# Interleaving the high and low rows of q and k in DRAM, and moving value tiles, one weight piece, zero fills and reflections in the order of work

## What is computed

```
x = x + gate * proj(attention(modulate(layernorm(x))))      # block 0, 16 heads of 18
x = x + gate * moe(modulate(layernorm(x)))                  # 4 experts, top 2 of them per token, hidden 1152, gelu
x = x + gate * attention(...);  x = x + gate * mlp(...)     # block 1: the same with one dense MLP
x_rot = x + ((x U) expm(A(cond)) - x U) U^T                 # block 2: U from qr(P), P 288 x 64; A skew-symmetric 64 x 64
x = x + gate * attention(...);  x = x + gate * mlp(...)     # block 3: layernorm with weights, exact gelu
```

## Time and profile before

| | us |
|---|---|
| median of 3 runs (lowest, highest) | 1743.58 (1736.67, 1746.56) |
| profiled execution | 1738.26 |
| its span | 1736.5 |
| PE busy | 1596.7 |
| DVE busy | 1095.3 |
| ACT busy | 942.5 |
| POOL busy | 607.3 |
| longest idle time of PE | 10.31, at 504 to 515 |

### The profile page before, as it was taken

How to read it: one execution, slowest core, us unless ns; L and a number is a source line. 1 busy time by engine, 2 the same in 40 slices (tenths; PEclk the granted TensorE clock), 3 DMA queues, 4 the chain that set the end, 5 groups by cost and what they waited for, 6 DMA issues and landing times.

```text
span 1736.5 us, 27878 instructions
## 1 busy us (share of the span) xinstructions
PE 1596.7 (92%) x9537; PEld 1040.5 (60%) x9537; DVE 1095.3 (63%) x2236; ACT 942.5 (54%) x1696; POOL 607.3 (35%) x1349
## 2 busy tenths in 40 slices
PE   7899989998979999997799999899988999998998
PEld 5334445446768888886335454489864354443897
DVE  4757777747535446564786877544447878784544
ACT  2456555566545455563365766744432667676442
POOL 1246576556245547554374742110001012101100
PEclk9789999899989999999699999999986999999999
DMA  6643434433464454441442222220203322222000
GB/s 193 189 133 102 149 112 156 140 129 103 163 207 131 147 179 149 158 145 46 147 127 84 85 66 86 73 60 1 47 27 114 107 82 90 70 83 73 18 28 28
DMA packets 101039, 183.44 MB, mean 106 GB/s; under 512 B 12141, under 2 KB 54520, under 8 KB 100786
## 3 DMA queue, kind: packets, MB, share of 16 engines
q1 hardware_dynamic: 90158, 145.97, 26.5%
q0 software_dynamic: 8352, 33.20, 6.1%
q10 hardware_dynamic: 2388, 2.48, 0.5%
HBM read 133.18 MB, written 60.05 MB: 111 GB/s over the span
## 4 chain that ended last, share of the span: by engine, by line
PE 67%; DVE 12%; DMA 8%; ACT 5%; issue 4%; POOL 2%; SPq 2%; DVEq 0%; ACTq 0%; POOLq 0%
PE ps L1328 14%; PE ps L1339 13%; PE ps L1186 7%; PE ps L1175 7%; PE ps L1064 6%; DVE mx L2036 5%; PE ps L1115 4%; PE ps L1162 3%; PE ps L1071 2%; DMA qk_rows<-qk 2%; PE ps L1104 2%; DMA w2raw<-in_w 2%; PE ps L1085 1%; PE ps L1078 1%; DMA qs<-nmT 1%
## 5 line engine op out<-in xcount | busy, mean ns | idle before, releaser
L2036 DVE TENSOR_REDUCE mx<-ps 128x1 f32<-128x512 f32 x768 | 481.5, 681 | 70.3 <-PE ps L1162 67.9
L1622 ACT ACTIVATE pT<-ps 128x512 f32<-128x512 f32 x768 | 410.1, 602 | 185.8 <-PE ps L1175 184.7
L1162 PE MATMUL ps<-ks,qs 54*128 54x512 f32 x768 | 299.3, 493 | 25.5 <-DMA ks<-qk_rows 16.2
L1175 PE MATMUL ps<-qs,ks 56*128 56x512 f32 x768 | 277.1, 463 | 14.9 <-DMA qs<-nmT 6.0
L1970 DVE TENSOR_TENSOR gl<-gf,gh 128x512 fp32r<-128x512 f32 x171 | 118.9, 696 | 194.0 <-ACT gh L1536 192.9
L1175 PEld LDWEIGHTS ps<-qs,ks 56*128 56x128 f32 x768 | 119.4, 192 | 178.8 <-issue 92.7
L1186 PE MATMUL ps<-pT,vaug 128*32 128x512 f32 x1536 | 214.4, 627 | 6.3 <-ACT pT L1622 6.3
L1339 PE MATMUL ps<-w2h,gh 128*128 128x288 f32 x684 | 206.5, 302 | 2.8 <-DVE tmpx L2070 1.9
L1339 PE MATMUL ps<-w2l,gh 128*128 128x288 f32 x684 | 201.8, 295 | 0.0
L1339 PE MATMUL ps<-w2h,gl 128*128 128x288 f32 x684 | 201.4, 294 | 0.0
L790 POOL TENSOR_SCALAR nwp<-mvp 128x4 f32<-128x4 f32 x21 | 4.1, 195 | 518.2 <-DVE mvp L1855 517.8
(11 more groups left out here) (293 smaller groups left out, 3044.3 us busy)
## 6 DMA issues: line engine op xcount, KB each, us to landing
qk_rows<-qk SPq DMA_DIRECT2D x96, 252.0 KB
w1raw<-in_w SPq DMA_DIRECT2D x39, 576.0 KB, 4.2
w2raw<-in_w SPq DMA_DIRECT2D x39, 432.0 KB, 4.9
qs<-qk_rows SPq DMA_DIRECT2D x96, 144.0 KB
ks<-qk_rows SPq DMA_DIRECT2D x96, 144.0 KB
expert_out<-expert_out POOLq DMA_DIRECT2D x8, 1152.0 KB, 7.1
htok<-expert_rows SPq DMA_DIRECT2D x11, 768.0 KB, 6.3
qs<-qk_rows SPq DMA_DIRECT2D x96, 72.0 KB
```

What stands on the lines that cost most here:

```text
L1162: ins = mm(bank(n), qs[at:at + KMAX, buf, h // 2, qt * P:(qt + 1) * P], ks[at:at + KMAX, buf, h // 2, :], start=True, stop=True, tile_posi ...
L1175: ins = mm(bank(n), ks[at:at + KROW, b % 2, h // 2, kt * P:(kt + 1) * P], qs[at:at + KROW, b % 2, h // 2, :], start=True, stop=True, tile_ ...
L1622: A(pT[:, kt % 2 * HG + i, :], bank(BANK[when[0], "score", (g, kt, i)]), ACT.Exp, scale=SCALE).then_inc(S["exp_done"], 1)
L2036: V.tensor_reduce(mx[:, g % NG, qt, column(i):column(i) + 1], bank(BANK[when[0], "max", (g, qt, i)]), AX.X, ALU.max).then_inc(S["mx_done"], 1)
```

## The change

The DRAM tensor `qk_rows` gets the shape heads x 18 x 2 x 512 in place of heads x 2 x 18 x 512: high and low row of one channel lie side by side. `rows_of` now names the rows of one part as one list with a fixed stride. `load_rows` takes, for `qs`, 36 interleaved rows and 18 high rows; for `ks`, the 18 high rows twice (into even and odd partitions) and the 18 low rows: with both halves of the partitions 10 DMAs per stack in place of 8, and `STACK_LOADS` (160) in place of 128 in the waits. At an opening the four value tiles stand between q/k tiles 1 and 2, on TensorE, on DVE and in the table of banks. For expert tile 3 the rows are loaded after the first weight piece, with the wait for the zero fills; two fills follow the first weight piece of tile 2, one each the second and the third. The reflections of expert tiles 7 and 10 move to other hidden tiles.

```diff
--- before.py
+++ after.py
@@ -54,7 +54,7 @@
 
 FWD_STEP = {(0, 0): (2, 5, 7, 9, 11, 14), (0, 1): (0, 2, 5, 7, 10, 12, 14), (0, 2): (0, 3, 5, 7, 10, 12, 14), (0, 3): (2, 5, 8, 11, 14),
             (1, 1): (0, 2, 4, 6, 9, 11, 13), (1, 2): (0, 2, 4, 6, 9, 11, 13)}
-FWD_TILE = ((3,), (), (0, 3, 6), (0, 3, 6), (0, 3, 6), (0, 3, 6), (0, 4), (2, 5), (0, 4), (0, 3, 6), (2, 5, 8))
+FWD_TILE = ((3,), (), (0, 3, 6), (0, 3, 6), (0, 3, 6), (0, 3, 6), (0, 4), (3, 7), (0, 4), (0, 3, 6), (1, 4, 8))
 
 
 def reflections_in(l, b):
@@ -99,7 +99,7 @@
 ROUTE_LATE = {(0, 5, "B"): [("T2", 0)], (0, 6, "B"): [("T2", 1)], (0, 7, "B"): [("T2", 2)], (0, 8, "B"): [("lg", 0)],
               (1, 0, "A"): [("back", 0)], (1, 0, "B"): [("back", 1)], (1, 1, "B"): [("lt", 0), ("top2", 0)], (1, 2, "A"): [("back", 2)],
               (1, 2, "B"): [("back", 3)], (1, 3, "B"): [("pos", 0)], (1, 4, "B"): [("list", 0)]}
-FILL_AT = ((0,), (1, 2), (3,))
+FILL_AT = ((0, 1), (2,), (3,))
 for i_, part_ in enumerate(MOD_PARTS):
     ROUTE_LATE.setdefault((3 + i_ // 4,) + ((1, "A"), (2, "A"), (2, "B"), (4, "B"))[i_ % 4], []).append(("M", (1,) + part_))
 for u_ in range(2):
@@ -194,10 +194,12 @@
         phase = ("start", l)
         for c in range(KC):
             take(phase, "T1", c)
-        for tile in range(QT - 1):
+        for tile in range(2):
             take(phase, "P", tile)
         for t in range(TT):
             take(phase, "V", t)
+        for tile in range(2, QT - 1):
+            take(phase, "P", tile)
         if l != 1:
             take(phase, "M", (l, 1))
             for u in range(2):
@@ -243,6 +245,7 @@
 KMAX = 3 * HD
 KROW = KMAX + 2
 HEAD = (1, 0, 3, 2)
+STACK_LOADS = 2 * 5 * 16
 
 
 def weights_at(j, first, last, ahead):
@@ -275,7 +278,7 @@
 def bass_cond_seq_kernel(nc, a, out):
 
     modd = nc.dram_tensor("mod_rows", [NL, B, MOD], F32).ap()
-    qkd = nc.dram_tensor("qk_rows", [2 * NH, 2, HD, N], F32).ap()
+    qkd = nc.dram_tensor("qk_rows", [2 * NH, HD, 2, N], F32).ap()
     wpd = nc.dram_tensor("proj_rows", [NL, C, C], F32).ap()
     vd = nc.dram_tensor("skew_rows", [B, RD * RD], F32).ap()
     hd = nc.dram_tensor("expert_rows", [IDLE * N, KC * P], F32).ap()
@@ -460,17 +463,21 @@
 
         def rows_of(tile, part):
 
-            return qkd[HT * tile:HT * tile + QR[tile] // HD, part], qk[0:QR[tile], tile % 2, part, :].bitcast(F32)
+            rows = qkd[HT * tile:HT * tile + QR[tile] // HD, :, part].rearrange("h d n -> (h d) n")
+            return rows, qk[0:QR[tile], tile % 2, part, :].bitcast(F32)
 
         def load_rows(eng, i, g, which):
 
             o = 2 * HG * g
-            for to, row, src in (((qs, 0, qkd[o:o + HG]), (qs, 2 * HD, qkd[o:o + HG, 0:1])),
-                                 ((ks, 0, qkd[o + HG:o + 2 * HG, 0:1]), (ks, HD, qkd[o + HG:o + 2 * HG])))[which]:
-                for e in range(2):
-                    part = src.rearrange("(p e) a d n -> e (a d) p n", e=2)[e]
-                    at = HALF * e + row
-                    eng.dma_start(to[at:at + part.shape[0], i % 2, 2 * g:2 * g + 2, :].bitcast(F32), part).then_inc(S[f"stack_ld{g}"], 16)
+            to, first = ((qs, o), (ks, o + HG))[which]
+            heads = qkd[first:first + HG].rearrange("(p e) d a n -> e d a p n", e=2)
+            for e in range(2):
+                high, low = heads[e, :, 0], heads[e, :, 1]
+                both = heads[e].rearrange("d a p n -> (d a) p n")
+                for at, step, src in ((0, 1, both), (2 * HD, 1, high)) if to is qs else ((0, 2, high), (1, 2, high), (2 * HD, 1, low)):
+                    rows = src.shape[0]
+                    start = HALF * e + at
+                    eng.dma_start(to[start:start + step * (rows - 1) + 1:step, i % 2, 2 * g:2 * g + 2, :].bitcast(F32), src).then_inc(S[f"stack_ld{g}"], 16)
 
         @block.sync
         def _(sp):
@@ -514,7 +521,7 @@
                     o = HT * tile
                     if i:
                         for g in range(o // (2 * HG), (o + QR[tile] // HD - 1) // (2 * HG) + 1):
-                            sp.wait_ge(S[f"stack_ld{g}"], i * 128)
+                            sp.wait_ge(S[f"stack_ld{g}"], i * STACK_LOADS)
                     for part in parts:
                         sp.wait_ge(S[("hi_done", "lo_done")[part]], i * QT + tile + 1)
                         sp.dma_start(*rows_of(tile, part)).then_inc(S[f"qk_st{tile % 2}"], 16)
@@ -656,9 +663,8 @@
                     load_projection(l + 1)
                 for k in range(1, TILES if l == 0 else 0):
                     if k > 1:
-                        if k == PICKED[2]:
-                            sp.wait_ge(S["zf_done"], NE * 16)
-                        load_tokens(k)
+                        if k != PICKED[2]:
+                            load_tokens(k)
                         e = expert_of(k)
                     if k > 1:
                         sp.wait_ge(S["gh_done"], NJ * (k - 1) + 3)
@@ -672,6 +678,9 @@
                         sp.wait_ge(S["fc1_mm"], NJ * (k - 1) + NJP * (q + 1))
                         sp.wait_ge(S["fc2_mm"], NJ * (k - 1) + NJP * (q + 1) + 3)
                         load_piece(w1, w2, q)
+                        if (k, q) == (PICKED[2], 0):
+                            sp.wait_ge(S["zf_done"], NE * 16)
+                            load_tokens(k)
                         for n in FILL_AT[q] if k == PICKED[2] - 1 else ():
                             sp.wait_ge(S["tl_ready"], 3)
                             sp.wait_ge(S["zb_ready"], 1)
@@ -1154,7 +1163,7 @@
                 def max_tiles(g, qt, which):
 
                     if qt == 0 and which[0] == 0:
-                        pe.wait_ge(S[f"stack_ld{g % NG}"], 128 * (it + g // NG + 1))
+                        pe.wait_ge(S[f"stack_ld{g % NG}"], STACK_LOADS * (it + g // NG + 1))
                     for i in which:
                         n = bank_free("max", (g, qt, i), "mx_done", G * NU + (NU * g + qt * HG + i + 1))
                         h = (g % NG) * HG + HEAD[i]
@@ -1253,10 +1262,12 @@
                     for c in range(KC):
                         turn_layernorm(1, c, it)
                     pe.wait_ge(S["wq_ready"], l + 1)
-                    for tile in range(QT - 1):
+                    for tile in range(2):
                         qk_tile(it, tile)
                     for t in range(TT):
                         v_tile(t)
+                    for tile in range(2, QT - 1):
+                        qk_tile(it, tile)
                     if l != 1:
                         if l == 0:
                             pe.wait_ge(S["ld_adar"], 32)
@@ -2114,11 +2125,13 @@
                     when[0] = ("start", l)
                     for c in range(KC):
                         split_h1(it, c)
-                    for tile in range(QT - 1):
+                    for tile in range(2):
                         low_part(it, tile)
                     dve.wait_ge(S["ld_w"], 16 * (l + 1))
                     for t in range(TT):
                         v_out(t)
+                    for tile in range(2, QT - 1):
+                        low_part(it, tile)
                     if l != 1:
                         modulation_half_out(l, 1, BANK[when[0], "M", (l, 1)])
                     if l == 0:
```

## The result

The kernel after took 1738.49 us (median of 20 runs, 1728.73 to 1745.49), the kernel before beside it 1744.9 us (20 runs, 1736.67 to 1757.28). The ratio is 0.996, 95% interval 0.9943 to 0.9977: 7.0 us faster (4.0 to 9.9), where 12.8 us had been forecast. The gain has the forecast's sign and the time lies in its range; the size was about half.

The account below looks back on a forecast made before the run. TensorE, busy 92% of the span, was taken to bound the kernel, so only its idle time could be saved. Gains of 2.5 + 2.0 + 0 + 6.0 + 2.3 = 12.8 us off 1743.58 gave 1730.8 us, range 1720 to 1741.

Parts of the forecast that it names:

- part 1: Stores of q/k rows: DMA share from 0.44 to about 0.88, landing 2.8 us earlier in the opening of layer 1.
- Rival 1: Stores of q/k rows get no faster, limited by something other than the number of engines: 1739.8 us; chance 0.13.
- part 2: Stack loads: 10 DMAs instead of 8, same bytes, cost SP 0.73 us more a stack; last load lands as much later.
- Rival 4: SP's queue: 35 us of extra issuing over 48 stacks makes it slower, 1752.7 us if 30 hand on delay; chance 0.07.
- Opening of layer 1, 2.5 us: First stack 2.1 us earlier (store -2.8, loads +0.73), second 0.4 more: 2.5 us gained.
- Elsewhere, 2.0 us: Waits for `nmT` and small stack waits outside layer 1's opening: chains 0.7 us shorter each, 2.0 us gained in all.
- Value tiles, 0: Value tiles between the q/k tiles at an opening: no gain and no cost.
- Expert tile, 6.0 us: Fourth expert tile: first weight piece issued 5.1 us earlier, rows landing just in time; 6.0 us gained.
- Rival 2: Rows of the fourth expert tile arrive last, turned at 510.3: gain 2.8 instead of 6.0 us, 1734.0 us; chance 0.12.
- Reflections, 2.3 us: Expert tile 7: the 3.82 us wait goes, 1.1 to 1.5 us come late next; gain 2.3 us, tile 10 nothing.
- Rival 3: More than the sum: shorter pauses leave TensorE's clock high and layer chains give all: 20 us, 1723.6 us; chance 0.13.
- Signs named beforehand: Wrong if the store's landing does not move, rows arrive after 508, or new waits for `nmT` appear in the layers.

Follow-up runs that it names:

- old_opening: Kernel after with the value tiles of an opening behind all q and k tiles again: 1717.8 us, 0.9904 of the kernel before on chip C.
- experts_only: Kernel before with only the fourth expert tile's edit, the zero fills and the moved reflections: 1731.3 us, 0.9986 of the kernel before on chip C.
- after_fourth: Kernel after, unchanged, run once more on chip E: 1715.1 us, 0.9878 of the kernel before.

## Why the prediction was wrong in size

**Stores (part 1): right.** Share 0.82 where 0.88 was expected, the landing 3.2 us nearer to the last issue where 2.8 was. From the last store's issue to the first load it is 2.5 us for 5.7; in the other profiles 2.6 to 3.1 us with the new rows and 4.7 to 5.8 with the old. Rival 1 (stores no faster) fell. By the section of the Trainium skill quoted there, "Why a DMA increments its semaphore by 16 and not by 1" in "DMA: Bandwidth & Descriptors", the share would be 14 of 16, 0.88, in place of 7 of 16, 0.44; the traces' 0.82 and 0.44 agree with it to 0.06.

**Loads (part 2): the price was mis-sized.** "2 x 0.37 = 0.73 us more" took the issue time of the old form for the new one. It is about 2.9 us a stack: 5.9 us for ten (1.41 + 4.44) against 2.94 for eight. The sum didn't suffer as feared, for two reasons: the opening's first wait ends with a landing that issuing doesn't set alone (5.51 us with cheap loads on chip E, 5.65 with dear ones; from the last load's issue to TensorE's start it was 3.66 us before and is 1.91 now), and stores give 0.9 us of SP a tile back. The wait for `nmT` near 127 us may be a trace of the price: 1.4 to 1.9 us in the eight profiles with ten loads, 0.5 to 1.7 in the four with six, 0 to 1.4 in the seven with the old rows. Rival 4 (SP's queue) fell, although its price was four times what it had assumed.

**Opening of layer 1, 2.5 us: right, with some luck.** The two waits fell by 4.4 us from the first profile of before and by 1.2 us on chip D (7.43 + 2.57 to 5.82 + 2.99). Over all profiles their sum is 10.9 us in the mean of the seven with the old rows and 8.5 in that of the twelve with the new: 2.4 us. From the last store's issue to TensorE's start it was 12.36 us and is 10.29, the -2.1 us of the first stack: 3.2 from the store in place of 2.8, and 1.15 lost on the loads in place of 0.73, because issuing doesn't set the pace alone. The prediction had named that ("less if the transfer does") and counted the whole of a price that was too low: two errors that cancel.

**Elsewhere, 2.0 us: too small.** It was bounded by the small waits of one profile that lacked the one at 187 us. The rows alone gave 8.2 us on chip B where 4.5 were forecast (2.5 + 2.0), and the whole against all but the rows gave 8.7 there. On the chips without pauses what is left for the rows is more: on C, old_opening against experts_only, 14.3 us; on E, 21.3 less 6.3 plus 0.5, 15.5 us, each good to 6 or 7 us.

**Value tiles, 0: not contradicted.**

**Expert tile, 6.0 us: right in size** (6.3 alone; 6.6 in the traces), though "the rows are just in time" failed: TensorE waits 3.58 us for them. The sum asked when ACT would be free for the rows, but TensorE turns them first and stood ready 3.58 us earlier. Rival 2's mechanism was there, the rows came last, at a smaller price: less the 9.3 us by which the execution was late, the first weight piece was issued at 496.1, as forecast, and TensorE turned the rows at 504.4, where rival 2 had 510.3.

**Reflections, 2.3 us: not there.** This is the term of the sum that failed: -0.5 us (-3.7 to 2.6) alone. The step in it is "With four steps of about 3.4 us instead of three the wait goes". The wait for POOL went; at hidden tile 7 TensorE then waits 2.40 us for DVE's `hTl`, which must empty the spare bank that the turn of rows has just filled, and tile 8 has the foreseen wait, 1.60 us. Together 4.0 us against 3.82. Tile 10, counted as nothing, lost 0.7.

**The sum.** Measured one by one the parts are 8.2 + 6.3 - 0.5 = 14.0 us, each with an error of 3 to 4; they come from two chips. The whole was 7.0 us on chip A and 13.2, 9.8 and 21.3 on B, D and E, mean 12.8. That this mean is the forecast is luck: a term too small (the rows) and one that wasn't there (the reflections) cancel in part. Of the 5.8 us missing on chip A the reflections account for 2.8 (2.3 forecast, -0.5 measured), while the rows, measured on B, gave more than forecast. What is left, 7 us between the sum of the parts and the whole, is as large as the error of that difference, and its cause is open.

No term of the sum had a difference between chips, and the runs show a large one: 7.0 to 13.2 us in A, B and D with pauses, 21.3 in E without. The last step of the sum took a median and one profile for the same thing ("the median of 1743.58, which lies 5.3 us above it"). That profile had no pauses and the fewest waits for rows of the seven with the old rows; the kernel after was profiled on chip A with 24 us more in the three stretches (17 after what is regained behind them) and still ended 4.2 us earlier. What isn't settled is why the chips with pauses take more from the new kernel: its median is 20 to 23 us higher on A, B and D than on E, that of the kernel before only 8 to 12 us. A part of a pause may hide under waits for rows that the new kernel no longer has; this is argued, not shown. Nor do pauses tell chip A's 7.0 us from the 13.2 of chip B, which has them too.

Rival 3 (more than the sum) is what chip E shows, 21.3 us, but not for its reason: TensorE's granted clock was still 0.50 of full speed (1.2 GHz) from 830 to 838 us of the kernel after, after a wait of 5.16 us, and from 817 to 829 us of after_fourth on chip E, after one of 5.65 us.

**Signs named beforehand.** The last sentence of the prediction listed new waits for `nmT` and rows after 508 as signs of its being wrong. The first came, at 1.70 us, but such waits fell from 6.0 to 4.0 us in all, and four of the six later profiles with the old rows have this one too, at 0.6 to 1.4 us. The second didn't: the rows at 513.67 are at 504.4 by the clock of the profile of before, less the 9.3 us by which the execution was late.

## What to carry to other kernels

Before one profile is made the base of a sum, take a second one of the same kernel on another chip: here two profiles of the kernel before differed by 12 us in the waits that the new rows were about, nearly three times what was forecast for the rows. And measure the change on more than one: it was worth 7 us on one chip and 21 on another. Price a DMA's issue by a DMA of the same form of addresses, not by its neighbour with the same bytes. When a wait for one engine is moved, look for what else falls due at the new place before counting it as gone.

## What the runs showed of the hardware

- SyncE's time to issue a DMA depends on its form of addresses: 0.32 or 0.75 us for loads of the same bytes, 0.77 or 0.32 us for the same store. A load that reads each row twice into 36 partitions in a row is as dear (0.744 us in the median) as one into 18 partitions, every second one (0.752 us); loads of 18 partitions in a row, and of 36 without doubling, take 0.32, and 0.48 right behind two dear ones. Why the form matters isn't settled.
- In all nine profiles of A, B and D, and in none of the nine of C and E, TensorE, VectorE and ScalarE fall behind together near 240 and 870 us (10 to 23 us in all against the first profile of before, with less near 335), while GpSimd goes on. In the kernel after on chip A:

```profile
243.24 0.96 POOL L839 DMA_INDIRECT expert_rows<-hrow,slot  x1 [0.30 <-issue]
...
245.28 0.46 DVE L2060 TENSOR_TENSOR vaug<-ps,vbias 128x288 f32<-128x288 f32 x1 [7.40 <-remote]
...
245.31 1.31 ACT L1633 ACTIVATE pT<-ps 128x512 f32<-128x512 f32 x2 [3.67 <-remote]
...
245.79 0.79 PE L1184 MATMUL ps<-qs,ks 56*128 56x512 f32 x1 [5.13 <-issue]
```

GpSimd's indirect DMAs are being issued in the stretches at 240 and 870 us in every trace, paused or not, so they alone don't make the pause; taking them away wasn't tried. From 236 to 248 us this trace has no packet of the queue that loads instructions, so nothing of such a load is seen in the pause, which doesn't rule it out. A neighbour on the chip wasn't looked for either. The cause is open.
